# Kernel study: the first mamba layer's weights in their own buffers, loaded by the first block

## What is computed

```python
x = x + L0_xattn(ctx, layernorm(x), in_proj_w, conv_w, conv_b, x_proj_w, dt_proj_w, dt_proj_b, A_log, D)
...   # layer 0 ffn, layers 1 and 2
x = x + L3_xattn(ctx, layernorm(x), ...)
x = x + L3_ffn(layernorm(x), ...)

def xattn(h, z, ...):                    # h: the context, z: the normed x
    xi = einsum('bld,ed->bel', h, in_proj_w)              # 256 -> 512 channels
    u = silu(causal_conv4(xi, conv_w) + conv_b)
    dt_lo, Bm, Cm = split(einsum('bdl,ed->bel', u, x_proj_w), [16, 32])
    delta = softplus(einsum('brl,dr->bdl', dt_lo, dt_proj_w) + dt_proj_b)
    A = -exp(A_log)                                       # 512 x 16
    # over the 512 steps: state = state*exp(delta*A) + delta*u*B ; y = sum(state*C)
    return (y + D*u) * silu(z)
```

## Time and profile before

| | |
|---|---|
| median of 3 runs | 4288.59 us (4285.73 to 4290.44) |
| profiled execution | 4288.35 us |
| its span, first to last instruction | 4286.6 us |
| mean granted TensorE clock | 0.926 |
| instructions | 46282 |
| busy: TensorE, VectorE, ScalarE, GpSimd | 84%, 69%, 41%, 36% |

### The profile page before, as it was taken

How to read it: one execution, slowest core, us unless ns; L and a number is a source line. 1 busy time by engine, 2 the same in 40 slices (tenths; PEclk the granted TensorE clock), 3 DMA queues, 4 the chain that set the end, 5 groups by cost and what they waited for, 6 DMA issues and landing times. The chain is left out here.

```text
span 4286.6 us, 46282 instructions
## 1 busy us (share of the span) xinstructions
PE 3607.8 (84%) x15168; PEld 1705.0 (40%) x15168; DVE 2941.3 (69%) x4121; ACT 1765.4 (41%) x2929; POOL 1535.4 (36%) x1070
## 2 busy tenths in 40 slices
PE   5788647999999999598999889775877777679898
PEld 2233214555555565342333344342332222234454
DVE  4888888577887773567887266447656888843663
ACT  4555322222222221243777253346645545321244
POOL 2999954112221120062000100014426999900122
PEclk8899878999999999797999989886988998989999
DMA  3455531133223212167663110010003544512420
GB/s 107 130 137 143 132 90 38 46 100 92 73 67 100 90 46 66 71 157 96 72 71 37 72 39 0 3 62 10 0 7 99 132 132 132 136 46 65 81 54 21
DMA packets 241368, 326.97 MB, mean 76 GB/s; under 512 B 40036, under 2 KB 141158, under 8 KB 240088
## 3 DMA queue, kind: packets, MB, share of 16 engines
q1 hardware_dynamic: 241160, 324.37, 30.9%
HBM read 276.33 MB, written 47.98 MB: 76 GB/s over the span
## 5 line engine op out<-in xcount | busy, mean ns | idle before, releaser
L521 POOL TENSOR_TENSOR m_dB<-m_du,m_BC 128x1024 f32<-128x1024 f32 x256 | 615.6, 2405 | 16.6 <-DVE m_du L553 16.6
L494 ACT ACTIVATE m_dA<-m_delta,m_a_neg 128x512 f32<-128x512 f32 x512 | 350.8, 690 | 486.5 <-DVE m_H_bank L588 419.7
L381 PE MATMUL m_y<-m_H,ident 128*128 128x512 f32 x512 | 294.2, 658 | 166.1 <-DVE m_H L599 166.0
L588 DVE TENSOR_TENSOR_SCAN m_H_bank<-m_dA,m_dB 128x512 f32<-128x512 f32 x256 | 315.0, 1230 | 127.9 <-POOL m_dB L521 103.6
L386 PE MATMUL m_y<-m_H,ident 128*128 128x512 f32 x512 | 293.4, 656 | 78.2 <-POOL m_H L506 78.2
L1631 DVE TENSOR_REDUCE a_core_minus_max<-a_core_a 128x1 f32<-128x512 f32 x512 | 317.1, 683 | 58.3 <-PE a_core_a L1457 58.3
L506 POOL TENSOR_TENSOR m_H<-m_H,m_BC 128x512 f32<-128x512 f32 x256 | 337.6, 1319 | 8.7 <-DVE m_H L593 7.9
L593 DVE TENSOR_TENSOR_SCAN m_H<-m_dA,m_dB 128x512 f32<-128x512 f32 x256 | 306.5, 1197 | 0.0
L1583 ACT ACTIVATE X<-a_core_s 128x512 f32<-128x512 f32 x512 | 264.5, 604 | 93.5 <-PE a_core_s L1457 93.4
L1023 POOL TENSOR_TENSOR ctxT<-ctxT,f_scales 128x1024 f32<-128x1024 f32 x48 | 107.0, 2228 | 532.3 <-DVE ctxT L848 532.3
L983 ACT ACTIVATE XN<-f_g,f_power_back 128x512 f32<-128x512 f32 x128 | 88.0, 687 | 402.9 <-PE f_g L920 402.9
(11 more groups left out here) (394 smaller groups left out, 7870.2 us busy)
## 6 DMA issues: line engine op xcount, KB each, us to landing
m_BC<-bc_rows SPq DMA_DIRECT2D x256, 512.0 KB, 4.8
XN<-in_L_ffn_w_dram SPq DMA_DIRECT2D x72, 256.0 KB, 2.7
ternary<-ctxT SPq DMA_DIRECT2D x96, 128.0 KB, 1.7
a_core_q<-a_q_parts SPq DMA_DIRECT2D x48, 256.0 KB, 12.8
a_core_k<-a_k_parts SPq DMA_DIRECT2D x48, 256.0 KB, 14.7
f_w_tern<-ternary SPq DMA_DIRECT2D x24, 512.0 KB, 6.4
f_core_q<-f_q_parts SPq DMA_DIRECT2D x24, 512.0 KB, 8.7
XN<-in_L_ffn_w_gate_dram SPq DMA_DIRECT2D x24, 256.0 KB, 2.7
```

Source lines behind the costliest of these rows:

```text
L381: pe.matmul(ps_y[:, 0, :], ident[:], HD[n % NH], start=False, stop=True, skip_group_check=True).then_inc(s_ad, 1)
L494: act.activation(dA[:, i % NA, :], delta[b % 2][:, e, :], ACT.Exp, scale=a_neg[:, e, k % N:k % N + 1]).then_inc(s_dA, 1)
L521: pool.tensor_tensor(dB[n % 2][:], du[b % 2][:, h * EH:(h + 1) * EH, :], BC[n % NS][:, 0:1, :].broadcast_to([P, EH, L]), ALU.mult).then_in ...
L588: dve.tensor_tensor_scan(ps_H[:], dA[:, 2 * n % NA, :], dB[n % 2][:, 0, :], 0.0, ALU.mult, ALU.add).then_inc(s_sc, 1)
```

## The change

A class `ScanWeights` holds buffers for the raw weights of a mamba layer, and the semaphore that their loads count up. Its `load` issues the same eight transfers in the same order. For layer 0 an object is made before the first stage; `stage_start` calls its `load` on SP between the context and x, and `stage_mamba` no longer issues loads. The raw in_proj_w, x_proj_w and dt_proj_w no longer lie in H and dB but in buffers of their own. For layer 3 an object is made right ahead of the stage, and the stage itself issues the loads at its start, as before, only into the new buffers. All waits for the semaphore stay where they are.

```diff
-def stage_start(chip, x, ctx_dram):
+class ScanWeights:
+
+    def __init__(self, chip, name, st, in_w, conv_w, conv_b, x_w, dt_w, dt_b, a_log, d_skip):
...
+        self.in_rows, self.x_rows = sb("in_rows", [P, self.EB, C]), sb("x_rows", [self.W, self.EB * P])
+        self.dt_rows, self.a_in = sb("dt_rows", [P, self.EB, self.R]), sb("a_in", [P, self.EB, self.N])
+        self.small = sb("small", [P, self.EB, self.TAPS + 3])
+        self.s_ld = chip.sem(name + "_weights_loaded")
+
+    def load(self, sp):
+        in_w, conv_w, conv_b, x_w, dt_w, dt_b, a_log, d_skip = self.dram
+        small, taps = self.small, self.TAPS
+        sp.dma_start(self.in_rows[:], in_w.rearrange("(e p) c -> p e c", p=P)).then_inc(self.s_ld, 16)
+        sp.dma_start(self.x_rows[:], x_w).then_inc(self.s_ld, 16)
+        sp.dma_start(self.dt_rows[:], dt_w.rearrange("(e p) c -> p e c", p=P)).then_inc(self.s_ld, 16)
+        sp.dma_start(small[:, :, 0:taps], conv_w.rearrange("(e p) c -> p e c", p=P)).then_inc(self.s_ld, 16)
+        for i, v in enumerate((conv_b, dt_b, d_skip)):
+            sp.dma_start(small[:, :, taps + i:taps + i + 1],
+                         v.rearrange("(e p o) -> p e o", p=P, o=1), allow_slow_non_contiguous=True).then_inc(self.s_ld, 16)
+        sp.dma_start(self.a_in[:], a_log.rearrange("(e p) c -> p e c", p=P)).then_inc(self.s_ld, 16)
+
+def stage_start(chip, x, ctx_dram, weights):
...
             sp.dma_start(cn[:], ctx_dram.rearrange("b (t p) c -> p (b t) c", p=P)).then_inc(s_c, 16)
+            weights.load(sp)
             sp.dma_start(X[:], x.rearrange("b (t p) c -> p (b t) c", p=P)).then_inc(chip.loaded, 16)
...
-def stage_mamba(chip, name, bc_dram, in_w, conv_w, conv_b, x_w, dt_w, dt_b, a_log, d_skip):
+def stage_mamba(chip, name, bc_dram, weights, load=False):
...
-        small = sb("small", [P, EB, TAPS + 3])
-        a_in, a_neg = sb("a_in", [P, EB, N]), sb("a_neg", [P, EB, N])
+        small, a_in, a_neg = weights.small, weights.a_in, sb("a_neg", [P, EB, N])
...
-        in_rows = H[:, 0:EH, :].rearrange("p e (h c) -> p (e h) c", c=C)
-        x_rows, dt_rows = H[0:W, EH, :], dB[0][:, 0, 0:EB * R].rearrange("p (e r) -> p e r", e=EB)
+        in_rows, x_rows, dt_rows = weights.in_rows, weights.x_rows, weights.dt_rows
...
-        s_ld, s_wt, s_wc = sem("loaded"), sem("w_transposed"), sem("w_copied")
+        s_ld, s_wt, s_wc = weights.s_ld, sem("w_transposed"), sem("w_copied")
...
-            sp.dma_start(in_rows, in_w.rearrange("(e p) c -> p e c", p=P)).then_inc(s_ld, 16)
...
+            if load:
+                weights.load(sp)
             for b in range(B):
...
-        chip.run(stage_start, a["x"], a["ctx_1024"])
-
-        chip.run(stage_mamba, "m0", bc, *mamba_args(a, "L0"))
+        with ExitStack() as held:
+            weights = ScanWeights(chip, "m0", held, *mamba_args(a, "L0"))
+            chip.run(stage_start, a["x"], a["ctx_1024"], weights)
+
+            chip.run(stage_mamba, "m0", bc, weights)
...
-        chip.run(stage_mamba, "m3", bc, *mamba_args(a, "L3"))
+        with ExitStack() as held:
+            chip.run(stage_mamba, "m3", bc, ScanWeights(chip, "m3", held, *mamba_args(a, "L3")), load=True)
```

More of the change, by code:

```diff
@@ L76, in run, with sb @@
         self.nc.all_engine_barrier()
-def stage_start(chip, x, ctx_dram):
+class ScanWeights:
+    def __init__(self, chip, name, st, in_w, conv_w, conv_b, x_w, dt_w, dt_b, a_log, d_skip):
+        self.EB, self.R, self.N, self.TAPS = in_w.shape[0] // P, dt_w.shape[1], a_log.shape[1], conv_w.shape[1]
+        self.W = self.R + 2 * self.N
+        self.dram = in_w, conv_w, conv_b, x_w, dt_w, dt_b, a_log, d_skip
+        def sb(n, shape):
+            return chip.sb(f"{name}_{n}", shape, F32, st)
+        self.in_rows, self.x_rows = sb("in_rows", [P, self.EB, C]), sb("x_rows", [self.W, self.EB * P])
[14 more added lines that the diff above has]
+def stage_start(chip, x, ctx_dram, weights):
     nc = chip.nc
@@ L203, in _ @@
             sp.wait_ge(chip.stored, 16 * B)
-def stage_mamba(chip, name, bc_dram, in_w, conv_w, conv_b, x_w, dt_w, dt_b, a_log, d_skip):
+def stage_mamba(chip, name, bc_dram, weights, load=False):
     nc, X, XN, ctxT, ident = chip.nc, chip.X, chip.XN, chip.ctxT, chip.ident
-    EB = in_w.shape[0] // P
+    EB, R, N, TAPS, W = weights.EB, weights.R, weights.N, weights.TAPS, weights.W
     EH = EB // 2
[L215 to L218, removed]
     NU = 2 * N
```

## The result

| | before | changed |
|---|---|---|
| median | 4290.51 us (9 runs, 4285.73 to 4293.83) | 4280.54 us (9 runs, 4276.94 to 4283.52) |
| profiled execution | 4288.35 us, span 4286.6 | 4283.52 us, span 4281.8 |

The ratio is 0.9975, with a 95% interval of 0.9965 to 0.9985: the changed kernel is 0.25% faster, 10.0 us between the medians. A second comparison gave 4281.12 against 4289.01 us, ratio 0.9981 (0.9972 to 0.9990). The forecast was 4280.6 us, a gain of 7.9 us.

What follows compares the result with a forecast made beforehand. With barriers between stages, each stage's length counts; the first mamba stage's start waited on weight loads. Terms -6.9 - 1.0 + 0 = -7.9 us, from between bases 4288.35 and 4288.59, gave 4280.6 us, range 4276.5 to 4286.5.

Steps and rivals of the forecast that it cites:

- Term 1, the wait: Start of the first mamba stage: the wait for weight loads goes, first work moves from 24.34 to 17.46, gaining 6.9 us.
- my bounds of 7.5 and 14.7: Start stage: weights landed by 7.5 us with nothing in front, by 14.7 if moving only after the context; needed by 17.46.
- Term 2, what the loads are moved in front of: SP's queue in the start stage: SP done between 8.8 and 16.9 us, x landing at 23.3, cost 0.
- Term 3, the clock: TensorE in the first mamba stage: weight transposes gain 1.0 us (bounds 0 and 1.6) at the high clock; projection gains 0.
- a rival at 10.2 us of gain: TensorE's clock stays up all through the first mamba stage's start: gain 10.2 us, total 4278.3 us; chance 0.25.
- The lid on this term: First mamba stage: TensorE also waits for VectorE's matrices, so the projection can't start before 21.9 us; gain at most 1.6.
- The signs of being wrong: A load wait before the weight transposes, context copies ending after 16.4 us, or a scan loop not 497.7 us long.
- The rest moves with it: Everything behind the projection shifts whole; scan loop keeps its 497.7 us pace, the last mamba stage changes by 0.
- Sharing with x: Start stage: weights share the engines with x, gain only 4.2 down to 1.0 us, total 4284 to 4287.5; chance 0.10.
- SP held: Start stage: SP, and the barrier with it, held at x's issue; if until 23.3 us, total 4288.4 us; chance 0.05.
- Slower scan loops: Both mamba stages: moved tiles slow the scan loops; at 2% slower the total is 4300.5 us; chance 0.05.
- 0.2% line: Whole kernel: 8.6 us separates a change from none; faster beyond it got 0.40, within it 0.55, slower 0.05.

Runs made afterwards that it cites:

- second profile: The changed kernel, unchanged, profiled once more: clock at 1.00 throughout, projection 7.11 us, first scan at 77.5 us.
- four profiles: Three profiles of the changed kernel and one with both mamba layers' loads early, sharing its start: first scan at 81.1 us in one, 77.2 to 77.5 in three.

## Why the prediction was right

The forecast of 4280.6 us met 4280.54 and 4281.12 us. The agreement to a tenth is luck, for the scatter is several us. And 7.9 us is the gain of neither course that the changed kernel takes: at the first scan, which I had put at 79.5 us, it is 6.35 us where the clock fell and 9.9 to 10.0 where it stayed up. What counts is the steps.

*Term 1, the wait.* Right in place and size. I had 24.34 - 17.46 = 6.9 us; the exponential came at 17.88 in the first profile (6.5 us) and at 17.46 in the second (6.9 us). The loads were in at 13.1, within my bounds of 7.5 and 14.7 and near the late one, 4.8 us ahead of need. Own buffers alone gave nothing and the loads with x ahead gave nothing, so it is the early issue behind the context, and ahead of x, that gains.

*Term 2, what the loads are moved in front of.* Right in its result, and short in one figure. SP was free at 12.05, between my 8.8 and 16.9, and x cost nothing, as VectorE still idled 26.45 us ahead of the log error. But x landed at 25.1 and not at 23.3, 5.0 us later than before: I had priced the loads by 3.2 us of busy engines, and not by the time that SP takes to issue them one after the other. x was issued only at 11.54, and the table by stretches has the engines all but empty from 11 to 12 us. The experiment with the loads ahead of the context bears this out, where the context is issued 5.0 us later and lands 5.1 us later. The place where I was nearly careless is the value 0 for SP being held. I argued from x's own issue of 2.18 us; the experiment with x first shows issues of 7.75 and 3.51 us. The order saved it, not the argument.

*Term 3, the clock.* The mechanism, a clock that can hold or fall at this place, was right; its weight was not. I gave 1.0 us for the weight transposes and 0 for the projection, with a rival at 10.2 us of gain if the clock stays up. In three of four profiles it did stay up: 87.42 - 77.49 = 9.9 us, just about the rival's 10.2. In the fourth, the first one, it fell at 18.5 us and rose in the projection: 87.42 - 81.07 = 6.35 us. The step that failed is the chance of 0.25 for that rival. I had counted the work between the two holes as too light to hold the clock, and in three profiles it was not. The Trainium skill, "TensorE: Matmul & The Clock Gate", section "HAM oscillation — how this bites in real kernels", which blames long gaps for the fall, was the better guide in three of the four profiles; the fourth speaks against it as the only cause, since TensorE's idle time ahead of the fall was 1.7 us and it fell while TensorE worked, and so does the same fall with the loads ahead of the context.
The lid on this term was real: in the second profile VectorE's matrices end at 21.58 + 0.28 = 21.86, in the same moment as ScalarE's last copy, 4.4 us after the exponential's start as I had worked out, and the projection starts at 21.96. And the small transposes, for which I had no row, start in pairs every 0.40 us at 1.00 against 0.58 at 0.50, so four pairs save 0.7 us.

*The signs of being wrong.* One of the three that I had named came up: in the first profile the copies of the context end at 16.84 and not by 16.4. It stood there for SP or the loads holding the stage up, and neither did; the clock had risen later, and in the second profile the copies end at 16.41. No wait for a load stands before the weight transposes, and the scan loop is 0.5 us off its 497.7.

*The rest moves with it.* Right: the scan loop took 497.2 us, and the shift at the first scan is there at the third stage (6.8 us). It does not show whole in the profiled executions, 4.8 us, as the middle stages took 2.0 us longer in the changed one's profile. I had taken the bases of the profiled run and of the median as 0.24 us apart; with more runs, the median of before rose by 1.9 us, to 4290.51.

*The rivals.* Sharing with x: out, the queue works in order. SP held: not in this order, but real in another. Slower scan loops: out. The two comparisons lie on both sides of the 0.2% line, at 0.25% and 0.19%, to which I had given 0.40 and 0.55. With the clock weighed as the profiles show it, faster would have had the larger share.

## What to carry to other kernels

Small loads at the head of a stage cost their issues and one flight: with nothing else in the queue 4.1 and 2.1 us here, for 686 KB. Moving all eight issues gained 6.5 to 6.9 us, and in a second stage of the same kind 6.5 more, while moving 93% of the bytes ahead of x, with five issues left behind it, gained 0.1. Put them in the queue behind the transfer that the current stage waits for and ahead of the large one that nobody waits for yet, and look how long each issue holds the issuing engine, since it has to reach the barrier too. Where a total scatters by as much as the effect, read marks in the timeline of several profiles, and give a clock that may or may not fall more than one profile.

## What the runs showed of the hardware

Most issues on SP take 0.4 to 0.5 us when nothing else is in flight (the load of D up to 1.0), but up to 7.75 us behind a context and an x that are still in flight. While the last of the small loads pass, the profile has the DMA engines' share at 1.30 with 104 GB/s between 10 and 11 us, and 2 GB/s in the us behind it, against 383 for x. The Trainium skill, "DMA: Bandwidth & Descriptors", section "Specifications", says that pieces below 512 B are written by reading and writing back; the low rate agrees with it, though no run here separates that from the cost of many packets, or from a queue that waits for SP's next issue. And the same program has the first 16 matmuls of its projection take 7.11 or 9.68 us from one execution to the next.
